# Transposing finished attention groups by DMA instead of on TensorE, in an eight-core transformer layer

## The reference

```python
xn = layernorm(x)
q, k, v = (xn @ w.T split into 16 heads of 128) for w in (q_w, k_w, v_w)
attn = softmax(causal(q @ k.T / sqrt(128)))
av   = attn @ v                                   # per head, tokens x 128
out  = av * sigmoid(q @ gate_w.T + gate_b)
x = x + layernorm(concat_heads(out) @ o_w.T)
h = layernorm(x)
x = x + layernorm(((silu(h @ g_w.T * g_s) * (h @ u_w.T * u_s)) @ d_w.T) * d_s)
```

## Time and profile before

| | us |
|---|---|
| median of 3 runs (1709.85 to 1791.71) | 1710.07 |
| the profiled execution | 1707.6 |
| its span on the slowest core, core 7 (role B) | 1705.8 |
| spans of the eight cores | 1703.3 to 1705.8 |
| TensorE busy on core 7 | 1653.5 |
| VectorE busy | 657.6 |
| ScalarE busy | 459.9 |

### The profile page before, as it was taken

One profiled execution on the slowest core, in us unless ns is written; L12 is line 12 of the kernel. 1 busy time (PEld: TensorE's weight loads), 2 busy tenths in 40 slices (PEclk: granted clock), 3 DMA queues, 4 the chain that ended last, 5 costly groups with the idle time before them and its releaser, 6 DMA issues.

```text
span 1705.8 us, 29447 instructions; the slowest of 8 cores (1703.3 to 1705.8 us)
## 1 busy us (share of the span) xinstructions
PE 1653.5 (97%) x11631; PEld 1053.4 (62%) x11631; DVE 657.6 (39%) x1406; ACT 459.9 (27%) x724; POOL 127.5 (7%) x245
## 2 busy tenths in 40 slices
PE   3899999999999999999999999999999999999997
PEld 2656666666666666665445555555555557888854
DVE  5946565655655656562662111111111110121135
ACT  3744444444444444444222111111111110000012
POOL 0000000000000000000000000000000021111100
PEclk9999999999999999999999999999999999999999
DMA  9832222222131313034338544454545477555557
GB/s 240 242 56 51 51 38 51 38 39 50 26 63 26 63 26 51 1 62 112 148 125 153 87 87 87 87 92 82 94 80 91 82 126 123 91 93 90 91 142 232
DMA packets 44065, 152.13 MB, mean 89 GB/s; under 512 B 5136, under 2 KB 6288, under 8 KB 39312
## 3 DMA queue, kind: packets, MB, share of 16 engines
q0 software_dynamic: 34704, 102.81, 35.5%
q1 hardware_dynamic: 9216, 47.33, 8.5%
HBM read 238.24 MB, written 14.68 MB: 148 GB/s over the span
## 4 chain that ended last, share of the span: by engine, by line
PE 91%; DVE 4%; issue 2%; DMA 1%; ACT 1%; DVEq 0%; ACTq 0%; SPq 0%
PE psum L359 91%; DVE st L389 2%; DMA xin<-x_l 1%; PE psum L364 1%; DMA b_yb<-y_d 0%; DVE psum L638 0%; DVE b_xb L956 0%; ACT mv L372 0%; DVE mv L391 0%; ACT b_h1b L425 0%; DVEq L1338 0%; DVE b_yb L1225 0%; DVE mv L376 0%; ACT b_yb L1219 0%; ACT b_h1T L453 0%
## 5 line engine op out<-in xcount | busy, mean ns | idle before, releaser
L359 PE MATMUL psum<-b_h2T,b_fw 128*128 128x384 bf16 (+1 forms) x2752 | 521.1, 352 | 0.0
L359 PEld LDWEIGHTS psum<-b_h2T,b_fw 128*128 128x128 bf16 x2752 | 269.2, 98 | 251.1
L359 PE MATMUL psum<-b_h1T,b_wb 128*128 128x512 bf16 (+1 forms) x1536 | 387.1, 370 | 0.4 <-DVE b_Bb L557 0.4
L645 ACT ACTIVATE b_P<-psum 128x512 bf16<-128x512 f32 (+1 forms) x368 | 217.9, 592 | 382.6 <-DVE psum L638 312.1
L638 DVE TENSOR_TENSOR psum<-psum,b_Bb 128x512 f32<-128x512 f32 (+2 forms) x480 | 236.3, 511 | 133.0 <-PE psum L359 130.2
L359 PE MATMUL psum<-b_wb,b_h1T 128*128 128x256 bf16 x2048 | 271.2, 274 | 0.0
L359 PE MATMUL psum<-b_wd,b_hdn 128*128 128x256 bf16 (+1 forms) x2200 | 268.5, 285 | 0.0
L359 PEld LDWEIGHTS psum<-b_wd,b_hdn 128*128 128x128 bf16 x2200 | 215.3, 98 | 53.2
L1046 DVE SCALAR_TENSOR_TENSOR b_hdn<-psum,cf,b_sg 128x512 bf16<-128x512 f32 (+1 forms) x88 | 60.2, 684 | 463.3 <-PE psum L359 462.0
L359 PEld LDWEIGHTS psum<-b_wb,b_h1T 128*128 128x128 bf16 x2048 | 193.6, 98 | 28.9
L359 PEld LDWEIGHTS psum<-b_h1T,b_wb 128*128 128x128 bf16 x1536 | 141.2, 98 | 105.1 <-issue 0.8
(11 more groups left out here) (84 smaller groups left out, 856.4 us busy)
## 6 DMA issues: line engine op xcount, KB each, us to landing
b_fw<-wg_d POOLq DMA_DIRECT2D x43, 512.0 KB, 5.3
b_fw<-wu_d POOLq DMA_DIRECT2D x43, 512.0 KB, 6.1
b_wd<-wd_d POOLq DMA_DIRECT2D x66, 256.0 KB, 3.7
xin<-x_l SPq DMA_DIRECT2D x15, 1024.0 KB, 7.8
b_wb<-wv_d POOLq DMA_DIRECT2D x16, 512.0 KB, 7.2
b_wb<-wk_d POOLq DMA_DIRECT2D x16, 512.0 KB, 5.9
b_wb<-wq_d POOLq DMA_DIRECT2D x16, 512.0 KB, 5.2
b_xb<-x_l SPq DMA_DIRECT2D x7, 1024.0 KB, 5.3
```

The costliest lines, as they stand in the source:

```text
L359: return self.q.do("T", lambda e: e.matmul(out, lhsT, rhs, start=start, stop=stop, skip_group_check=True), waits, tok)
L645: te = self.q.do("S", lambda e: e.activation(p[:, 0:128 * n], self.bank(b, 128 * n), ACT.Exp, scale=CSC), [ta, self.av_tok.get(gi - PRING)])
```

## The change

In heads 0 to 14 a finished group is no longer transposed by TensorE. `close` issues, right behind the normalising of `avn`, one DMA with transpose on SP's queue, from `avn` to a new tile `avT` of chip memory (two slots, like `avn`). The job that is left is the gating alone; it reads `avT` in place of bank 5 and is due seven ticks later in place of three. The loop at the start of `close` now waits for the gating job of the group two before to have been emitted, and not for its transposes. Head 15 keeps the old way.

```diff
-    def dma(self, chan, dst, src, waits=()):
+    def dma(self, chan, dst, src, waits=(), turn=False):
...
-        self.put(chan[0], lambda e: e.dma_start(dst, src), w, lane, 16)
+        self.put(chan[0], (lambda e: e.dma_start_transpose(dst, src)) if turn
+                 else (lambda e: e.dma_start(dst, src)), w, lane, 16)
...
+        self.avt_free = {}
...
+        self.avT = [sb(f"avT{i}", [128, 3, 128], BF16, r.AVT_AT + 768 * i)
                     for i in range(2)]
...
-        while k >= 2 and k - 2 not in self.avn_tr:
+        while k >= 2 and k - 2 not in self.avt_free:
             self.small.pop(0)[3]()
...
+        c = slice(128 * x, 128 * (x + n))
+        th, avT = self.th[h % 2], self.avT[k % 2]
+        if h < H - 1:
+            self.avn_tr[k] = q.dma("Y", avT[:, 0:n, :],
+                                   avn[:, 0:n, :].rearrange("p t c -> p (t c)"),
+                                   [ev, self.avt_free.get(k - 2)], turn=True)
+
+            def job():
+                tg = q.do("V", lambda e: e.scalar_tensor_tensor(
+                    self.gat[:, h, c].rearrange("p (t c) -> p t c", c=128),
+                    th[:, c].rearrange("p (t c) -> p t c", c=128), 1.0,
+                    avT[:, 0:n, :], ALU.add, ALU.mult),
+                    [self.avn_tr[k], self.tok["th", h]])
+                self.avt_free[k] = self.gat_tok[h] = tg
+            self.small.append(("v", h, self.now + 7, job))
+            return
+
         def job():
             for i in range(n):
                 t = self.tr(self.bank(5)[:, 64 * i:64 * i + 64].bitcast(BF16),
                             avn[:, i, :], [ev] + self.bf[5], tok=(i == n - 1))
             self.avn_tr[k] = t
...
-            self.gat_tok[h] = tg
+            self.avt_free[k] = self.gat_tok[h] = tg
         self.small.append(("t", h, self.now + 3, job))
```

More of the change, by code:

```diff
@@ L134 @@
     F_AT = [160768, 162816]
-    P_AT, AVN_AT, ABSQ_AT = 175104, 181248, 182784
+    P_AT, AVN_AT, ABSQ_AT, AVT_AT = 175104, 181248, 182784, 185088
     H1B = 36864
@@ L160 @@
     F_AT = [181248, 183296]
-    P_AT, AVN_AT, ABSQ_AT = 181248, 187392, 105472
+    P_AT, AVN_AT, ABSQ_AT, AVT_AT = 181248, 187392, 105472, 188928
     H1B = 107520
@@ L228, in memory @@
         self.avn = [sb(f"avn{i}", [128, 3, 128], BF16, r.AVN_AT + 768 * i)
+                    for i in range(2)]
+        self.avT = [sb(f"avT{i}", [128, 3, 128], BF16, r.AVT_AT + 768 * i)
                     for i in range(2)]
@@ L695, in job @@
             self.avn_tr[k] = t
-            c = slice(128 * x, 128 * (x + n))
-            th, src = self.th[h % 2], self.bank(5, 64 * n).bitcast(BF16)
+            src = self.bank(5, 64 * n).bitcast(BF16)
             tg = q.do("V", lambda e: e.scalar_tensor_tensor(
```

## The result

The changed kernel takes 1723.1 us (median; 1722.5 to 1723.7) against 1710.05 us: ratio 1.0074, 95% interval 1.0055 to 1.0093. It is slower, by less than 2%, and 3 us beyond the range given. The profiled execution took 1723.1 us.

What follows compares the result with a forecast made beforehand. TensorE was taken to bound the kernel: -6.0 us removed, 0 for heads 0 to 13, 5 - 2.6 added at head 14's end, sum -3.6 us; from 1710.07 to 1706.5 us, range 1702 to 1720.

Steps and rivals of the forecast that it cites:

- What bounds it, what is removed: TensorE sets attention's time; removing role B's seven transposes a head saves 0.40 us in each of 15 heads, 6.0 us.
- Role B sets the time: Role A's slowest core ended 1.1 us before core 7 and gains more, so role B keeps setting the time.
- L in the clear: Time from the end of VectorE's normalising to the transpose's landing, without competing transfers: taken as 4 us.
- the transfers of SP and POOL overlap twice: Casts meet transposes in every second head, idle again before the limit, and at 774 to 778, where it is tight.
- L = 5 at 774: Landing time taken for head 14's first group, beside casts: 5 us, 2.4 over what is free there.
- an end of 13.8: Upper end for a transpose's landing: 7.1 us for small pieces, plus another 6.7 us beside casts.
- the rule of one microsecond on TensorE for each above 2.6: End of head 14: every microsecond of landing time over 2.6 us costs TensorE one, once.
- The limits of steady heads, 7.3 and 7.1 us: Heads 0 to 13: groups one and two may land this late after normalising before TensorE loses time.
- The slower one: Rival: VectorE waits for the crossbar in every head; +80 us at a 10 us landing; chance 0.09 beyond 2%, 0.03 short.
- The load of x: Output projection, tile 1: moves behind SP's last transposes to about 778.7, lands by 784, read at 822.62; no cost.

Runs made afterwards that it cites:

- 13 heads: Against the kernel before: heads 0 to 12 transposed by DMA, heads 13 and 14 on TensorE; 1703.59 us, repeated 1703.51 us, ratio 0.9972.
- 14 gave: Against the kernel before: heads 0 to 13 by DMA, head 14 on TensorE, head 13's gating jobs due after 20 ticks; 1703.0 us, repeated 1702.28 us.
- casts held back: Changed kernel, with output-weight casts issued in heads 14 and 15 also waiting for the last transpose of head 13 or 14; 1706.54 us.
- rows: Changed kernel with the transpose replaced by a plain copy in rows of 768 bytes; one time, 1713.6 us.
- head 14 alone: Against the kernel before: only head 14 transposed by DMA, all other heads on TensorE; 1719.18 us, ratio 1.0067.
- copy by pieces: Changed kernel with the transpose replaced by a plain copy in pieces of 256 bytes; lowest of three times 1722.0 us.

## Why the prediction was wrong

- **What bounds it, what is removed: right.** A steady head went from 45.09 to 44.71 us where 44.7 was forecast; 13 heads gave 4.8 to 5.8 us for 5.2, 14 gave 6.1 to 6.4 for 5.6.
- **Role B sets the time: right**, for another reason than the 1.1 us: each core of role A met only one late landing, of 7.8 to 7.9 us, beside two casts (509.86 to 510.93 on core 0), and lost 2.9 to 3.0 us of TensorE to it.
- **L in the clear: mis-sized, without effect.** 4 was taken, 2.4 is measured, below the 3.1 kept as lower end.
- **The step "the transfers of SP and POOL overlap twice": wrong.** Only every second head and the stretch from 774 were weighed. The trace of before had a third place, four casts issued in one go at the start of head 14, just ahead of head 13's groups two and three. On the timeline of GpSimd on core 7 before, with the normalising of group two at 741.88:

```profile
739.32 2.11 POOL L97 DMA_DIRECT2D b_wb<-wo_d  x4 [63.25 <-PE psum L359]
```

They fill the engines for some 10 us, from 742 to 752, where the pairs of the earlier heads were over before the limit. This stall, 7.8 us, was in no sum.
- **The term "L = 5 at 774": mis-sized, and decisive.** The working held the right mechanism and its price, a cast's packet of 0.28 us between any two of about 25 an engine, 6.7 us on top of 7.1, an end of 13.8. It was then left aside for a round number near the plain loads. Measured: 12.7. That the end of 13.8 lies so near is in part luck: its base of 7.1 took a small packet at 0.25 us of an engine, where 251 of them at 55.9% in 0.5 us make 0.02, and a wait of some 4 us before the first packet was not in it. With the rule of one microsecond on TensorE for each above 2.6, that term is 10.1 instead of 2.4; measured 10.3 of waiting. The rule itself held: landings of 3.6, 7.7, 12.7 and 13.2 us (casts held back, rows, the change, head 14 alone) went with waits of 1.2, 5.4, 10.3 and 10.9.
- **The limits of steady heads, 7.3 and 7.1 us: not contradicted, but used in the wrong place.** On core 3 VectorE waited once 2.0 us, at 565.47, for a landing of 6.8, and on core 7 four times before 732, 4.9 us in all; TensorE waited for nothing there. But beside head 14's units no values are left to project (`fillers`) and the units are shorter: from group two of head 13 to that of 14 before were 35.7 us (741.88 to 777.56) in place of 45.09. There a wait of 6.2 us at VectorE became 6.0 at TensorE: no slack.
- **The clock was not in the sum.** Some 2.5 us after each stall at 1.2 GHz. With it, -6.0 + 6.0 + 10.3 + 2 x 2.5 is +15.3; core 7's span grew by 14.3, the median by 13.0.
- **The rivals.** The slower one had the right waiting engine and the right chain behind it, but every head for its place. What happened is its mechanism at two heads only, which falls between it and the forecast, and the range of 1702 to 1720 ended 3 us short. (The chances of what lies within 2% add to 0.91, where 0.90 is written.)
- **The load of x** for tile 1 went out at 792.68 and not at 778.7, since the transposes ahead of it on SP were late; it still cost nothing.

The Trainium skill's table of transpose paths ("VectorE: DVE Perf Modes") gives 1309 ns for one tile by the crossbar. The estimate from it, 3.9 us for three, was above the 2.4 measured in the clear and far under the 12.7 beside casts. Its preference for TensorE was right here for heads 13 and 14 with the gating job due after seven ticks, and wrong by 0.4 us a head for the others.

## What to carry to other kernels

A small transfer between two instructions is priced not by its bytes but by its packets, times a packet of whatever else the engines are moving when it is issued, and here some 4 us before its first packet: list every burst of the other queue beside every place of the new transfer, the irregular last ones above all. Where it may land late, move its reader in the program's order, not the transfer: the same late landing cost 8 us or nothing by the date of the job that waits for it. And a slack read off a steady loop holds for that loop; at its end, where units are shorter, read it again.

## What the runs showed of the hardware

- Two queues on the same DMA engines took turns packet by packet, whatever the packets' size (256 or 768 bytes against some 3.5 KB): 112 to 112 in 2 us for the transpose, 106 to 106 for the copy by pieces, 111 to 112 for that by rows (744 to 746).
- A transfer issued into a burst of four or five casts moved no packet for 3 to 4.5 us before the turns began, where in the clear it starts after 1.1 us: asked for at 736.1, first packets from 740; at 775.9, from 780; the copy by rows at 738.0, from between 741 and 742. So it is not the crossbar's either. Why so long is open: no run varied it.
- A crossbar transpose of 128 x 384 bf16 landed in 2.3 to 2.4 us in the clear, 1.2 of it SP's issue; the median of plain copies of as many pieces was 2.1.
